# A graph network kernel whose third pass reads its target one-hots back from DRAM, where the second pass has stored them

## The chip, the cores and the metric

The kernel runs on one core of a Trainium2 chip. The metric is the device time of one execution in microseconds (us), smaller is better. The core has five engines that run side by side and wait for each other by semaphores only: TensorE (PE in the profile, its weight loads PEld), VectorE (DVE), ScalarE (ACT), GpSimd (POOL) and SyncE (SP), which here only issues DMAs. Transfers between SBUF and DRAM run on 16 DMA engines that all queues share.

## What is computed

Four layers of a graph network follow each other on 12500 nodes of 32 features and 212500 edges, sorted by target. Each layer normalises the node rows, and sums rows of the edges' sources, weighed, at the edges' targets:

```python
h = relu(layernorm(x))
# layer 0
msg = (h @ W_rel)[src, edge_type_16] * edge_weight1
x = x + segment_sum(msg, dst)
# layer 1: two propagations with the same edge weights
prop(v) = segment_sum((-dinv[dst] * edge_weight * dinv[src])[:, None] * v[src], dst)
Tx1 = prop(h);  Tx2 = 2 * prop(Tx1) - h
x = x + relu(h @ W[0] + Tx1 @ W[1] + Tx2 @ W[2] + b)
# layer 2: attention over edges, with a matrix for each of 86 edge types
x = x + relu(segment_sum(a[:, None] * msg, dst) + self_loop)
# layer 3: mean over the neighbours
x = x + segment_sum(h[src], dst) / max(deg, 1)
```

A row of features is 32 numbers. The two `prop` calls of layer 1 have the same sources, targets and weights; only the rows that they pick differ.

## The kernel before

There are five passes over the edges, `s` = 0 to 4 in the code: the first (layer 0), the second and third (the two propagations of layer 1), the attention pass (`s` = 3) and the last (`s` = 4, layer 3). An edge group has 1024 edges, and there are 208 groups. In the second, third and last pass a part of the groups is not gathered but handled as sorted blocks; the others are gathered row by row.

**Sorted blocks.** The first pass sorts 4 groups (4096 edges) at a time by source into 49 buckets of 256 nodes with room for 128 edges ("slots") each. The second and third pass have 26 such blocks, the last has 39. A block is worked off in 8 batches, one of 7 buckets and seven of 6. I call the work on one batch a step: 26 x 8 = 208 steps in the second pass and 208 in the third. In a step `q`

- SP spreads the slots' source numbers over 128 partitions (`lows`, 224 or 192 KB, a ring of 4);
- DVE compares them with the partition's number (`compare_sources`, two instructions), which gives a one-hot for each source;
- PE multiplies that one-hot with the node rows (`pick`), each row kept as three bf16 parts; it runs some steps ahead;
- DVE weighs the picked rows by the edges' weights, and DVE and ACT split the result again into three bf16 parts (high part on ACT, remainder on DVE, middle part on ACT, last part on DVE, in a chain over three steps);
- DVE compares each bucket's targets with 0 to 255 (`compare_targets`, one instruction of 128x256 bf16 for each bucket, 6 or 7 in a step). This gives `to_oh`, a one-hot of the target inside the block's window of 256 nodes, in a ring of 2;
- PE multiplies the split rows with `to_oh` (`send`), and sums over the block in PSUM. After the block's 8 batches DVE adds the 96x256 sums to `big` in SBUF (`add_block`).

**Gathered groups.** For the other 104 groups of the second and third pass GpSimd issues indirect DMAs, 8 for each group of 1024 edges, so 832 in a pass, into 4 slots. Four groups belong to each block; batches 0, 2, 4 and 6 name them:

```python
HIDDEN = {s: {0: 0, 2: 1, 4: 2, 6: 3} for s in (1, 2)}
```

DVE weighs a gathered group and compares its targets (`weigh_group`), PE multiplies (`multiply_group`), DVE adds the window's 80 columns to `big` and frees the slot (`add_group`, whose wait is for PE's last multiplication of that group). ACT lays out the next row numbers as soon as a group has landed.

**Order around the change.** The order of each engine's instructions is written out by hand. In the DVE's step `q` of `pick_weighed` (line 1847 on) it was: sources of batch `q+1`, [third pass, `q` = 2: `add_block`], weigh batch `q`, targets of batch `q-1`, remainder of `q-1`, last part of `q-2`, then

```python
if q - 1 in HIDDEN[s]:
    weigh_group(s, i, HIDDEN[s][q - 1], f=f)
if q - 2 in HIDDEN[s]:
    add_group(s, i, HIDDEN[s][q - 2], f)
```

PE's order in the step that belongs to it is: a piece of the table for the attention pass (third pass only), `pick` of a later batch, `multiply_group`, `send`. So the group that DVE adds at the end of a step is multiplied on PE behind a `pick` that waits for `compare_sources` at the start of the same DVE step.

The third pass also builds that table: as soon as nodes are complete, DVE normalises a pair of node tiles (lines 1982 to 2012), PE makes the products, ACT copies them out and stores 544 or 495 KB a piece (two for each step) from its own queue. SP's queue has only the spread source numbers during a pass. The last pass is like the second with another splitting (no weights), three blocks for a turn, and its own `pick_turn`.

## Time and profile before

| | |
|---|---|
| median of 3 runs | 7773.39 us (7771.03 to 7800.02) |
| the profiled execution | 7774.41 us, of it 7772.6 us span |
| busy: POOL / DVE / PE / ACT | 5242.6 / 4897.8 / 4872.0 / 2357.4 us |
| second pass (DVE's first to last step) | 2331 to 3404 us |
| third pass | 3466 to 4793 us, then the last table pieces to 4873 us |
| attention pass | 4873 us to about 6960 us |
| last pass | 7025 to 7728 us |

How to read the profile: busy time is the time in which an engine executes; idle time before an instruction is put down to what released it. "issue" is time in which the engine waited for nothing that the profile shows, such as its own register and branch instructions. DVEq is DVE's instruction queue: "DVEq L1574" is the semaphore that `add_group` raises when a slot is free. PEclk is the clock that TensorE was granted as a share of 2.4 GHz. Lines are those of the kernel before: L1806 `compare_sources`, L1813 `compare_targets`, L1823 and L1827 `add_block`, L1554 and L2016 `weigh_group`, L1580 `add_group`, L1223 and L1226 `pick`, L1112 `multiply_group`, L1239 `send`, L712 the gathers, L1042 the table stores, L486 the extra semaphore instruction of a double wait.

### The profile page before, as it was taken

The numbers are of one execution on the slowest core, as the hardware profiler recorded it, in microseconds if no ns is written. First come the engines' busy times: TensorE is split into PE (matmuls) and PEld (weight loads), VectorE is DVE, ScalarE is ACT, GpSimd is POOL, SyncE is SP. The second block draws the span as 40 slices with busy tenths as digits, with TensorE's granted clock in tenths as the row PEclk, the third lists the DMA queues.
The fourth block names the chain that finished last, engine by engine and source line by source line (L and its number), as shares of the span: only waits on it lengthen the run. The fifth ranks groups of instructions, "written<-read, shape, count | busy, mean of one in ns | idle before, by whom it ended". The sixth has DMA issues, their size and how long they took to land.

```text
span 7772.6 us, 149728 instructions
## 1 busy us (share of the span) xinstructions
PE 4872.0 (63%) x41375; PEld 4126.7 (53%) x41376; DVE 4897.8 (63%) x16081; ACT 2357.4 (30%) x7420; POOL 5242.6 (67%) x5417
## 2 busy tenths in 40 slices
PE   5333333333337667677777776777777777786777
PEld 2222222222225555566666665677777776775666
DVE  5555555567778888866666665444444444449997
ACT  4444444430012222223544445211121212123322
POOL 2777777777747777757665662677777777756663
PEclk6555555555556776767776776555555555558998
DMA  7111111110012222224656666222222222214443
GB/s 171 14 14 14 14 14 14 14 14 13 13 22 53 52 52 52 52 44 143 213 190 203 201 198 205 59 41 41 41 41 41 41 41 41 41 34 94 100 100 79
DMA packets 464811, 547.95 MB, mean 70 GB/s; under 512 B 217753, under 2 KB 373945, under 8 KB 464629
## 3 DMA queue, kind: packets, MB, share of 16 engines
q0 software_dynamic: 173168, 146.14, 12.7%
q1 hardware_dynamic: 235013, 186.26, 9.4%
q10 hardware_dynamic: 56448, 213.62, 7.0%
q8 instruction: 53, 0.87, 0.0%
q14 instruction: 129, 1.06, 0.0%
HBM read 298.88 MB, written 246.72 MB: 70 GB/s over the span
## 4 chain that ended last, share of the span: by engine, by line
POOL 33%; DVE 21%; issue 18%; PE 17%; DVEq 8%; DMA 2%; ACT 1%; POOLq 0%; ACTq 0%; SPq 0%
POOL arena L712 33%; DVE tbuf L1813 6%; PE ps_agg L1112 6%; DVE tbuf L1806 3%; PE ps_agg L1239 2%; DVEq L1858 2%; DVEq L1561 2%; PE ps_wide L1223 1%; DVE msg L1857 1%; DVE H L1813 1%; DVE msg L1860 1%; PE ps_wide L1342 1%; PE ps_wide L1226 1%; DMA arena<-table,ibuf 1%; DVEq L1863 1%
## 5 line engine op out<-in xcount | busy, mean ns | idle before, releaser
L712 POOL DMA_INDIRECT arena<-table,ibuf x3328 | 3151.3, 947 | 1242.4 <-issue 1129.9
L712 POOL DMA_INDIRECT arena<-nodes,ibuf x2080 | 2088.6, 1004 | 1142.9 <-issue 616.2
L1112 PE MATMUL ps_agg<-mem_b,arena 128*32 128x80 f32 (+1 forms) x3744 | 457.6, 301 | 504.0 <-DVEq L1561 497.7
L1112 PE MATMUL ps_agg<-mem_a,arena 128*32 128x80 f32 (+1 forms) x3744 | 433.0, 291 | 533.0 <-DVEq L1561 511.0
L1112 PEld LDWEIGHTS ps_agg<-mem_b,arena 128*32 128x32 f32 (+1 forms) x3744 | 400.1, 152 | 554.1 <-DVEq L1561 520.9
L1112 PEld LDWEIGHTS ps_agg<-mem_a,arena 128*32 128x32 f32 (+1 forms) x3744 | 378.9, 146 | 592.6 <-DVEq L1561 528.9
L1813 DVE TENSOR_SCALAR tbuf<-iota,at_f 128x256 bf16<-128x256 bf16 x3185 | 680.9, 297 | 0.3 <-PE ps_t L1239 0.3
L1377 PE MATMUL ps_agg<-tbuf,msg 128*64 128x80 f32 x2496 | 373.6, 344 | 337.9 <-DVE msg L2039 337.9
L983 ACT ACTIVATE att<-score 128x8 f32<-128x8 f32 x208 | 43.3, 208 | 1649.1 <-DVE score L2030 1649.1
L1377 PEld LDWEIGHTS ps_agg<-tbuf,msg 128*64 128x64 f32 x2496 | 336.0, 227 | 359.0 <-DVE msg L2039 359.0
L835 ACT ACTIVATE tbuf<-O,tbuf 128x49 bf16<-128x49 bf16 x1664 | 448.5, 363 | 78.3 <-DVE H L1728 78.3
L1580 DVE TENSOR_TENSOR big<-big,ps_agg 32x80 f32 (+1 forms) x468 | 108.2, 231 | 570.5 <-PE ps_agg L1112 555.9
L1806 DVE TENSOR_SCALAR tbuf<-idx_a,pcol 128x768 bf16<-128x768 bf16 (+1 forms) x1040 | 398.9, 425 | 61.1 <-issue 43.2
L2022 DVE TENSOR_TENSOR msg<-arena,ps_z 128x256 f32<-128x256 f32 x208 | 87.6, 421 | 548.6 <-DMA arena<-table,ibuf 548.6
L1239 PE MATMUL ps_t<-tbuf,mem_b 128*96 128x256 bf16 x1560 | 275.4, 325 | 227.5 <-DVE mem_b L1874 176.8
L1239 PE MATMUL ps_t<-tbuf,mem_a 128*96 128x256 bf16 x1625 | 263.2, 307 | 203.9 <-DVE big L1827 108.8
L1372 PE MATMUL ps_wide<-yw,mem_b 80*128 80x33 f32 x1680 | 380.6, 403 | 1.2 <-ACT yw L965 1.2
L1372 PE MATMUL ps_h<-yw,mem_b 80*128 80x33 f32 x1664 | 377.0, 403 | 0.0
L1372 PEld LDWEIGHTS ps_wide<-yw,mem_b 80*128 80x128 f32 x1680 | 366.4, 330 | 19.1 <-issue 17.8
L1372 PEld LDWEIGHTS ps_h<-yw,mem_b 80*128 80x128 f32 x1664 | 362.9, 330 | 17.7 <-issue 17.7
L1554 DVE TENSOR_TENSOR arena<-arena,ew_s 128x256 f32<-128x256 f32 x416 | 176.5, 424 | 308.6 <-DMA arena<-table,ibuf 295.4
L1239 PEld LDWEIGHTS ps_t<-tbuf,mem_b 128*96 128x96 bf16 x1560 | 192.5, 144 | 260.1 <-DVE mem_b L1874 190.4
(388 smaller groups left out, 11745.8 us busy)
## 6 DMA issues: line engine op xcount, KB each, us to landing
table<-tbuf ACTq DMA_DIRECT2D x294, 544.5 KB
idx_a<-lows_d SPq DMA_DIRECT2D x637, 192.0 KB
arena<-table,ibuf POOLq DMA_INDIRECT x3328, 2.4
table<-tbuf ACTq DMA_DIRECT2D x98, 495.0 KB
arena<-nodes,ibuf POOLq DMA_INDIRECT x2080
table<-tbuf SPq DMA_DIRECT2D x25, 1024.0 KB, 4.3
idx_a<-lows_d SPq DMA_DIRECT2D x91, 224.0 KB
nodes<-O SPq DMA_DIRECT2D x7, 224.0 KB, 3.0
```

Source lines behind the costliest of these rows:

```text
L712: nc.gpsimd.indirect_dma_start(out=INTO[s][:, k, c, 0:WIDTH[s]], out_offset=None, in_=TABLE[s], in_offset=bass.IndirectOffsetOnAxis(ap=ibu ...
L835: op = nc.scalar.mul(moved[:, j, 2 + part, :], by_bucket[:, j, :], of)
L1112: last = nc.tensor.matmul(ps_agg[ROW0[s]:ROW0[s] + CHN[s], 0:WIN], narrow[:, k, c, 0:CHN[s]], onehots[b][:, c, :], start=(c == 0), stop=(c ...
L1239: last = nc.tensor.matmul(block_sums[s][0:SPLIT, 0:W2], slot_rows[q % 2][:, k, :], to_oh[s][q % 2][:, k, :], start=(b0 + k == 0), stop=(b0 ...
L1372: last = nc.tensor.matmul(y_own[b][:, c, :], onehot_t[:, c, :], yw[:, :], start=True, stop=True)
L1377: last = nc.tensor.matmul(ps_agg[0:2 * D, 0:WIN], msg[:, c, :], onehots3[k][:, c, :], start=(c == 0), stop=(c == CH - 1))
L1554: V.tensor_tensor(rows, rows, by[:, of].unsqueeze(2).to_broadcast([P, CH, D]), ALU.mult)
L1561: dve.drain()
L1580: V.tensor_tensor(into, into, ps_agg[r0:r1, 0:WIN], ALU.add)
L1806: op = V.tensor_scalar(from_oh[s][q % 2][:, a, 0:n * CAP], lows[q % RING][:, 0:n * CAP], pcol2[:, a:a + 1], None, ALU.is_equal)
L1813: op = V.tensor_scalar(to_oh[s][q % 2][:, k, :], iota2[:, :], at_f[:, e % UNIT[s], b0 + k:b0 + k + 1], None, ALU.is_equal)
L1858: dve.drain()
```

## The change

1. **Second pass: the one-hots are kept.** SP stores every batch of target one-hots to DRAM (`targets_d`), 448 or 384 KB each, 83.5 MB in all, behind the spread of the source numbers 6 batches later (`keep_targets`). DVE waits, before it overwrites one of the two buffers, until the store from it has landed.
2. **Third pass: they come back.** DVE's `compare_targets` and the loading of target numbers (`start_block`) are gone there. SP loads the batch from DRAM into one of the two buffers when PE has sent the batch two before (`return_targets`), and `send` waits for the load (`s_there`).
3. **Second and third pass: order on DVE.** `add_group` moves from step `q-2` to step `q-3`, and ahead of `weigh_group` in that step; `add_block` of the third pass moves from the start of step 2 to behind the remainders (in the second pass it moves ahead of `weigh_group` only). Where no group is weighed, a `drain` stands.
4. **Last pass.** Nothing is read back (`RETURNED` is empty). The one-hots have a ring of 4 in another tile, and the three blocks of a turn are 13 apart instead of neighbours. The order on the engines stays.

The core of the diff:

```diff
+KEPT = BLOCKS[1]
+TO_RING = {1: 2, 2: 2, 4: 4}
+RETURNED = ()
...
+    targets_d = scratch("targets_d", (KEPT * P, NBK * W2), BF16)
...
-        to_oh = {s: [onehot_piece(s, 2 + j).rearrange("p (k w) -> p k w", w=W2) for j in range(2)] for s in BLOCKS}
+        to_oh = {s: [onehot_piece(s, 2 + j).rearrange("p (k w) -> p k w", w=W2) for j in range(2)] for s in (1, 2)}
+        to_oh[4] = [O[:, at:at + n].bitcast(BF16).rearrange("p (k w) -> p k w", w=W2)
+                    for at, n in ((0, 896), (896, 768), (1664, 768), (2432, 768))]
...
+        def block_of(s, n):
+            turn, e = divmod(n, UNIT[s])
+            return e * TURNS[s] + turn
...
-            def spread_lows(h):
-
-                with sp.Fori(0, BLOCKS[(1, 2, 4)[h]]) as i:
-                    for q, (b0, n) in enumerate(BATCHES):
-                        sp.wait_ge(s_from, (BEFORE[h] * NBATCH + q + 1) + i * NBATCH)
-                        sp.dma_start(lows[q % RING][:, 0:n * CAP],
-                                     lows_d[bass.ds(i * (NBK * CAP) + b0 * CAP, n * CAP)].partition_broadcast(P)).then_inc(s_bc[q % RING], 16)
+            def spread_low(h, i, e, q):
...
+            def keep_targets(i, f, q):
+
+                sp.wait_ge(s_made, (f * NBATCH + q + 1) + i * NBATCH)
+                sp.dma_start(kept_rows(i, f, q), to_oh[1][q % 2][:, 0:BATCHES[q][1], :].rearrange("p k w -> p (k w)")).then_inc(s_kept[q % 2], 16)
+
+            def return_targets(h, i, e, q):
+
+                s = (1, 2, 4)[h]
+                sp.wait_ge(s_sent, ((BEFORE[h] + e) * NBATCH + q + 3 - TO_RING[s]) + i * (UNIT[s] * NBATCH))
+                sp.dma_start(to_oh[s][q % TO_RING[s]][:, 0:BATCHES[q][1], :].rearrange("p k w -> p (k w)"),
+                             kept_rows(i, block_of(s, e), q)).then_inc(s_there[q % TO_RING[s]], 16)
+
+            def spread_and_keep():
+
+                late = 6
+
+                def block(i, f, first=False):
+                    for q in range(NBATCH):
+                        spread_low(0, i, f, q)
+                        if q >= late:
+                            keep_targets(i, f, q - late)
+                        elif not first:
+                            keep_targets(i, f - 1, q - late + NBATCH)
...
+            def spread_and_return(h, ahead, soon, returned):
...
+                def turn(i, f, last):
+                    for m in range(n):
+                        if m + ahead < n or not last:
+                            spread(i, f, m + ahead)
+                        if m + soon < n or not last:
+                            give_back(i, f, m + soon)
...
-            spread_lows(0)
+            spread_and_keep()
             store_nodes(1, 1, lambda i: ubuf[1][i])
-            spread_lows(1)
+            for j in range(2):
+                sp.wait_ge(s_kept[j], 16 * (KEPT * NBATCH // 2))
+            spread_and_return(1, 5, 0, (0,))
...
-            spread_lows(2)
+            spread_and_return(2, 4, 2, RETURNED)
...
                     if q == 0:
                         pe.wait_ge(s_sbadd, (BEFORE[h] + e + 1) + i * UNIT[s])
                         carry_wait(pe)
+                    if s == 2:
+                        pe.wait_ge(s_there[q % 2], 16 * (e * (NBATCH // 2) + q // 2 + 1) + i * (16 * NBATCH // 2))
+                        carry_wait(pe)
...
                 def compare_targets(i, e, q):
                     b0, n = BATCHES[q % NBATCH]
-                    dve.wait_ge(s_sent, count(i, e, q, 1))
+                    dve.wait_ge(s_sent, count(i, e, q, 3 - TO_RING[s]))
+                    if s == 1 and (e > 0 or q > 1):
+                        dve.wait_ge(s_kept[q % 2], 16 * ((e * NBATCH + q) // 2) + i * (16 * NBATCH // 2))
+                        carry_wait(dve)
                     for k in range(n):
...
-                        if s == 2 and q % NBATCH == 2 and (q >= NBATCH or not first):
-                            add_block(i, f + q // NBATCH - 1)
                         if q < NBATCH:
                             dve.wait_ge(s_got, count(i, f, q, 3))
...
-                        if goes(q - 1):
+                        if s == 1 and goes(q - 1):
                             compare_targets(i, f, q - 1)
                         dve.drain()
...
+                        if q % NBATCH == 2 and (q >= NBATCH or not first):
+                            add_block(i, f + q // NBATCH - 1)
+                        if q - 3 in HIDDEN[s]:
+                            add_group(s, i, HIDDEN[s][q - 3], f)
+                        if q == 1 and not first:
+                            add_group(s, i, SLOTS - 1, f - 1)
                         if q - 1 in HIDDEN[s]:
                             weigh_group(s, i, HIDDEN[s][q - 1], f=f)
-                        if q - 2 in HIDDEN[s]:
-                            add_group(s, i, HIDDEN[s][q - 2], f)
-                        if q == 0 and not first:
-                            add_group(s, i, SLOTS - 1, f - 1)
-                        if s == 1 and q % NBATCH == 2 and (q >= NBATCH or not first):
-                            add_block(i, f + q // NBATCH - 1)
+                        else:
+                            dve.drain()
...
+                    for j in range(2):
+                        dve.wait_ge(s_kept[j], 16 * (KEPT * NBATCH // 2))
                     dve.wait_ge(s_own, 1)
```

**The order on DVE in the third pass.** First the steps 2 and 3 of a block in the loop of the third pass, on DVE, before: from the weighing of batch 2 (L1860) to the group's window (L1580).

```order
L1860 ISA
L1860 TENSOR_TENSOR msg<-ps_wide,slot_ew 128x192
L1813 TENSOR_SCALAR H<-iota,at_f 128x256 x6
L1869 TENSOR_TENSOR msg<-msg,mem_b 128x192
L1874 TENSOR_TENSOR mem_a<-msg,mem_a 128x7x32
L486 ISA
L486 TENSOR_LOAD meta
L1563 REGISTER_ALU
L1580 REGISTER_ALU
L1580 ISA
L1580 TENSOR_TENSOR big<-big,ps_agg 32x80
```

The same step on DVE in the changed kernel, whose line numbers are others (L1944 weighs, L1953 and L1958 are the remainder and the last part, L1908 adds the block):

```order
L1944 ISA
L1944 TENSOR_TENSOR msg<-ps_wide,slot_ew 128x192
L1953 TENSOR_TENSOR msg<-msg,mem_b 128x192
L1958 TENSOR_TENSOR mem_a<-msg,mem_a 128x7x32
L1902 REGISTER_ALU
L1902 TENSOR_LOAD block_i
L1908 ISA
L1908 TENSOR_TENSOR big<-big,ps_agg 32x256 x3
```

The six target comparisons are gone, the block's sums stand behind the last part instead of at the start of the step, and the group's window is no longer here. It stands a step later, ahead of the next group's weighing; step 3 on DVE in the changed kernel:

```order
L1944 TENSOR_TENSOR msg<-ps_wide,slot_ew 128x192
L1953 TENSOR_TENSOR msg<-msg,mem_a 128x192
L1958 TENSOR_TENSOR mem_b<-msg,mem_b 128x6x32
L495 ISA
L495 TENSOR_LOAD meta
L1652 REGISTER_ALU
L1662 REGISTER_ALU
L1662 ISA
L1662 TENSOR_TENSOR big<-big,ps_agg 32x80
```

**The order on SP in the third pass.** Two steps of the loop before, on SP: one spread of source numbers for each step.

```order
L675 ISA
L675 DMA idx_a<-lows_d 128x896
L674 REGISTER_ALU
L675 ISA
L675 DMA idx_a<-lows_d 128x768
```

The first two steps of the loop now, on SP (L688 is the spread, L706 the load of one-hots into H):

```order
L688 ISA
L688 DMA idx_a<-lows_d 128x768
L705 REGISTER_ALU
L706 ISA
L706 DMA H<-targets_d 128x1792
L687 REGISTER_ALU
L688 ISA
L688 DMA idx_a<-lows_d 128x768
L705 REGISTER_ALU
L706 ISA
L706 DMA H<-targets_d 128x1536
```

Each step now has a second DMA with a wait of its own on SP; the source numbers run 5 batches ahead of the load that stands behind them.

## Rows read from the trace of the kernel before

**Rows 1.** The page's chain of waits over the whole span, shares by engine.

```profile
POOL 33%; DVE 21%; issue 18%; PE 17%; DVEq 8%; DMA 2%; ACT 1%; POOLq 0%; ACTq 0%; SPq 0%
```

**Rows 2.** Busy time by stretch; columns as in the first line. Rows in order of time.

```profile
core 0: us, PE busy (x) PEld busy (x) DVE busy (x) ACT busy (x) POOL busy (x), PEclk, DMA share, GB/s
2331.00:3404.00 1073.00, 754.44 (x5988) 613.45 (x5985) 914.57 (x2881) 241.18 (x1044) 810.51 (x826) 0.71 0.25 51
3466.00:4793.00 1327.00, 976.20 (x13903) 826.07 (x13907) 901.35 (x3280) 607.44 (x1837) 803.55 (x820) 0.73 0.60 190
4793.00:4873.00 80.00, 34.42 (x263) 28.22 (x255) 24.04 (x45) 39.38 (x109) 0.00 (x0) 0.50 0.55 219
4900.00:6900.00 2000.00, 1578.34 (x8224) 1414.84 (x8223) 881.05 (x3005) 392.91 (x1050) 1511.77 (x1603) 0.50 0.22 41
7025.00:7728.00 703.00, 509.12 (x6574) 439.64 (x6575) 667.70 (x2726) 207.58 (x364) 447.44 (x409) 0.98 0.44 98
```

**Rows 3.** Who waited for whom in the third pass; us in total, times, longest.

```profile
POOL arena L712 <- DVEq L1574: 244.5, 84, 4.9
POOL arena L712 <- issue: 236.2, 736, 1.9
...
PE ps_wide L1223 <- DVE H L1806: 183.1, 68, 7.4
DVE big L1580 <- PE ps_agg L1112: 159.1, 79, 2.9
...
PE ps_agg L1239 <- DVE mem_b L1874: 66.5, 58, 4.2
...
PE ps_h L1337 <- ACT ht L1018: 50.3, 46, 2.1
...
DVE big L1823 <- PE ps_agg L1239: 24.7, 10, 4.0
...
PE ps_agg L1239 <- DVE mem_a L1874: 20.1, 25, 1.4
```

**Rows 4.** The chain of waits in the third pass, shares by engine and line.

```profile
by line: issue 12.6%; PE ps_agg L1112 11.7%; PE ps_agg L1239 11.1%; PE ps_wide L1223 8.6%; DVE H L1813 7.3%; PE ps_wide L1342 5.1%; DVE H L1806 3.9%; DVEq L491 2.7%; DVE msg L1860 2.6%; PE ps_wide L1346 2.5%; PE ps_t L1342 2.3%; DVEq L1561 
```

**Rows 5.** Groups of instructions in the third pass, the target comparisons.

```profile
L1813 DVE TENSOR_SCALAR H<-iota,at_f 128x256 bf16<-128x256 bf16 x1274 | 271.3, 298 | 0.0
```

**Rows 6.** Waits in the second pass, POOL's and DVE's.

```profile
POOL arena L712 <- issue: 250.8, 823, 0.3
...
DVE tbuf L1806 <- issue: 35.1, 103, 0.7
...
DVE big L1827 <- issue: 19.6, 25, 0.8
DVE big L1580 <- PE ps_agg L1112: 19.1, 42, 1.1
```

**Rows 7.** Timeline at the end of the second pass: last gather, last weighing.

```profile
3391.96 1.01 POOL L712 DMA_INDIRECT arena<-nodes,ibuf  x1 [0.30 <-issue]
...
3397.30 0.42 DVE L1554 TENSOR_TENSOR arena<-arena,ew_s 128x256 f32<-128x256 f32 x1
```

**Rows 8.** DMA queues in the third pass (q10 ACT, q1 SP, q0 POOL): packets, MB, share.

```profile
q10 hardware_dynamic: 51840, 196.19, 37.7%
q1 hardware_dynamic: 55888, 41.79, 13.3%
q0 software_dynamic: 26272, 13.50, 8.8%
```

**Rows 9.** The page's DMA issues: KB each, median us from issue to landing.

```profile
table<-tbuf SPq DMA_DIRECT2D x25, 1024.0 KB, 4.3
...
nodes<-O SPq DMA_DIRECT2D x7, 224.0 KB, 3.0
```

**Rows 10.** Timeline of the third pass: one send of six buckets on PE.

```profile
4011.57 1.49 PE L1239 MATMUL ps_agg<-H,mem_b 128*96 128x256 bf16 x6
```

**Rows 11.** The gathers from issue to landing, over the whole run.

```profile
DMA to landing us min/median/max: 2.2/2.4/6.2
```

61 lines of the change are left out of this document (47 added, 14 removed).

## The prediction, made before the changed kernel ran

> **What bounds the kernel now.** I began with the page's chain of waits [rows 1]: POOL has a third of it, so the gathers set much of the span. But this is a mean over passes. The busy time by stretch [rows 2] separates them: in the attention pass nothing of the change is present, and I leave it; the second, third and last pass are the ones it touches.
>
> In the third pass (3466 to 4793, 1327 us for 208 steps, 6.38 us a step) no engine is full: PE 976, DVE 901, POOL 804, ACT 607 us busy, the DMA engines 0.60 [rows 2]. The waits [rows 3] show a loop between PE and DVE. DVE waits 159.1 us for PE's group multiplication before it can add the window (L1580), and 24.7 us for the last send before it adds the block (L1823). PE in turn waits 183.1 us for `compare_sources` (L1806), which DVE reaches only after that addition, and 66.5 + 20.1 us for the split rows. POOL waits 244.5 us for DVE to free a slot. The chain of this stretch [rows 4] agrees: PE lines, DVE's L1813 with 7.3%, and no POOL line among the shares printed.
>
> In the second pass (1073 us) POOL is the one that never stops: 823 of its pauses are "issue" of 0.3 us, 250.8 us in total [rows 6], and no wait for a slot stands against them. A gather takes 810.51 / 826 = 0.981 us [rows 2] and the pause 250.8 / 823 = 0.305, so 832 gathers need 1069 us of 1073. DVE is nearly full too: 915 us busy, and short gaps of its own. At the end of the pass [rows 7] the last gather is issued by 3392.97; with a landing of 2.4 us [rows 11] its rows are there at 3395.4, and DVE weighs them at 3397.3. DVE is 1.9 us behind POOL after a whole pass, so neither has anything to give.
>
> In the last pass DVE is busy 667.7 of 703 us [rows 2], and is the bound.
>
> **The third pass, part by part.** Removed on DVE: 1274 comparisons, 271.3 us [rows 5], 1.3 us a step. Moved: `add_group` a step later. Its wait was for a multiplication that stood on PE behind the `pick` of the same step; a step later PE is past it, so most of the 159.1 us goes. `add_block` behind the remainders has more time for PE's last send, and most of the 24.7 us goes; the first send of the next block waits for it, but in the step in which DVE did it before, too, only a few instructions later. Taken singly this is the chain's 7.3% of 1327, 97 us, and 184 us of waits: 281 us. That is more than can be had, since other engines become late next. What each needs for the pass:
>
> - POOL: 832 gathers. At the third pass's 803.55 / 820 = 0.980 us [rows 2] and 0.305 between, 1069 us. In the attention pass, which has no bf16 comparisons on DVE, a gather takes 1511.77 / 1603 = 0.943 us, in the last pass, which is dense with them, 447.44 / 409 = 1.094 [rows 2]. With half the comparisons gone the need is therefore between 832 x 1.248 = 1038 and 1069. I take 1069.
> - PE: 1327 less the waits for DVE (183.1 + 66.5 + 20.1), 1057 us, at the granted clock of 0.73 [rows 2]; the 50.3 us for ACT [rows 3] stay in it. The new wait on `s_there` adds a semaphore instruction to each send, counted below.
> - DVE: 1327 - 159.1 - 24.7 - 271.3 = 872 us. It is no longer near.
> - DMA: 0.598 x 1327 = 794 us of all 16 engines now [rows 8]. ACT's queue moves 196.19 MB in 37.7% of 1327, 500 us, 392 MB a ms; SP's 41.79 MB in 13.3%, 176 us, 237 MB a ms, in smaller packets. The 83.5 MB that come back cost 213 us at the first rate and 352 at the second: 1007 to 1146 us. The returned rows are 3 and 3.5 KB, like the table's 3.8 KB (196.19 MB in 51840 packets), so I take 1007.
>
> The slot that is freed a step later (5 us) does not stop POOL: it comes back to a slot after three other groups, 3 x 8 x 1.285 = 31 us after it filled it, and the slot is busy for landing (2.4), the wait for its turn, and two steps more, some 20 us.
>
> So the pass can't be shorter than 1069 us, 258 less than now. It won't be exactly that: PE and POOL are then equally full, with DVE's uneven steps between them (the pair of tiles is normalised in two steps of four). The two passes with one full engine show what lies between the need and the time: 1073 / 1069, 0.4%, in the second, and 703 / 667.7, 5%, in the last. With two full engines and busy DMAs I take 6%: 1133 us, **194 us less** (5.45 us a step). The bounds are 258 less, and, if only the comparison leaves the chain, 97 less.
>
> The load itself is hidden in this: it is issued when PE has sent batch m-2 and wanted at send m. From the page, 224 KB land in 3.0 us and 1024 KB in 4.3 [rows 9], so 384 or 448 KB in 3.3. If two table stores of 544 KB are in flight, 1.1 MB at 392 MB a ms is 2.8 us before it; with the source numbers (0.8 us at their rate) it lands in about 7 us. Two steps of 5.45 less a send of 1.5 [rows 10] leave 9.4.
>
> **The second pass.** Added on DVE: in 206 of 208 steps a second wait and a semaphore instruction, and a drain in the steps without a group, four more a block, 104 in all. The trace has no row for one alone. The pause before L1806, where a double wait, a semaphore and a drain meet, is 35.1 / 103 = 0.34 us [rows 6]; so one costs between 0 and 0.34, 0 to 70 us. I take 0.1 for a wait (21 us) and 0.05 for a drain (5 us); both are nearer to the lower end, since 206 waits at 0.34 would be 70 us of pause, twice the whole of that row. Removed: the 19.1 us in which DVE waited for the group's product [rows 6]. The sum is **7 us more**; at best POOL allows 2 us less, at worst, with the full 0.34, it is 70 - 19 + 5 = 56 more. The stores take 213 us of DMA beside a share of 0.25 x 1073 = 268: not near full. One is issued when its comparison is done and has to land two steps later, 10.3 us less 1.3 for the comparison between; 3.3 us is what it needs. DVE's last wait for the stores, and SP's before the third pass, cost about 1 us: SP stores the node rows before it waits.
>
> **The last pass.** The waits are for other semaphores with the same partners, and the ring of 4 lets DVE compare before a send whose end it doesn't have to wait for: 0 us, since DVE's own work is the bound and none of it is removed. 35 us of slack (703 - 667.7) is all that could be found there, and the same for a loss.
>
> **The sum**, against the profiled execution's own 7774.4 us (its span and 1.8 around it; the median of the runs is 7773.4, 1 us below): 7774.4 - 194 + 7 + 1 = **7588 us**.
>
> **Rivals.**
>
> 1. *Gathers alone pace the third pass.* For it: POOL sits in 244.5 us of waits that all end in DVE. Then 1069 us, 258 less: 7524. Against: PE's 1057 leave it nothing. If PE's clock rises from 0.73 because its pauses shorten, as in the last pass (0.98), this is what comes.
> 2. *The DMA engines fill up.* At SP's rate the need is 1146 us, and with 5% between need and time 1203: 124 less, 7658. For it: 0.60 now with peaks above; against: the long rows.
> 3. *The comparison was cover, and only its own share of the chain goes*, because DVE then waits for PE elsewhere (for the high part, or at `pick`): 97 less, 7685.
> 4. *The returned one-hots come late, and the kernel is slower.* The place is the wait before `send`. Two steps can't be shorter than a landing and a send, L + 1.5. Today two steps are 12.76, so the third pass loses from L = 11.3 us on; each further us costs 104. At L = 12.5 a step is 7.0 us, the pass 1456, 129 more, and the kernel 7774.4 + 129 + 8 = 7911. For it: gathers landed in up to 6.2 us at worst where the median is 2.4 [rows 11], so landings can stretch 2.6-fold, and 3.3 would be 8.6. Against: 8.6 is still below 11.3.
>
> The Trainium skill speaks for rival 4 ("DMA: Bandwidth & Descriptors", Queues, rings and completion order): a DMA's completion is written only after every earlier write of the same DMA engine, those of other queues included. By that rule a load counts as landed only when the table stores before it are written, and a second pair of stores in flight would add another 2.8 us to the 7. No row of the kernel before shows a large load beside large stores, and this by itself would not reach 11.3.
>
> **Chances.** The forecast 0.45, rival 1 0.15, rival 2 0.18, rival 3 0.12, rival 4 0.07; 0.03 for a third pass as now and the second pass's cost on top. A difference below 0.5% (39 us) can't be told from none here. Faster by more: 0.88, from the first four less a little where the costs of the second pass meet rival 3; within: 0.04; slower: 0.08. The range reaches to the times of rivals 1 and 3 and leaves out rival 4: 7520 to 7695.
>
> **What would show it.** In the changed profile: the third pass from 1327 to about 1133 us, with DVE near 640 us busy, no L1813 in it, and the wait of `add_group` for PE below 30 us. POOL's wait for slots falls from 244.5 to some 50. The second pass stays at 1073 to 1085, with POOL still never waiting. DMA share in the third pass near 0.9, in the second near 0.45. If PE's wait before `send` is put down to a DMA for more than 50 us, rival 2 or 4 has it; if DVE's waits for PE come back at another line, rival 3. The sum is wrong in its second term if DVE's gaps in the second pass grow by more than 30 us, and in its first if POOL waits for slots as before.

## The result, and the profile after

The changed kernel takes **7706.9 us** (median of 4 executions, 7705.3 to 7711.0), the kernel before 7784.7 (4 executions, 7771.0 to 7800.0): ratio 0.9905, 95% interval [0.9891, 0.9919]. The two profiled executions (7774.4 and 7708.5) are 66 us apart, where 186 were forecast, and the time lies above the range. The direction was right, the size was not.

Where the 66 us are. A pass is measured from the start of its first comparison to the end of its last block sum, in us. Each length here and below comes from one profiled execution of its kernel, and whole executions of one kernel differ by more than 20 us (the kernel before: 7771.0 to 7800.0), so a difference of about 10 us in one pass is weak evidence by itself.

| | before | after | change | forecast |
|---|---|---|---|---|
| second pass | 1075.6 | 1088.4 | +13 | +7 |
| third pass | 1327.4 | 1219.7 | **-108** | -194 |
| last pass | 695.7 | 720.8 | **+25** | 0 |
| all between them | | | +4 | +1 |

The busy time of the same stretches after, with the columns of [rows 2] (window, PE, PEld, DVE, ACT, POOL, PEclk, DMA share, GB/s); second, third and last pass:

```profile
2331.00:3419.00 1088.00, 775.72 (x6002) 639.00 (x6001) 925.82 (x2882) 240.98 (x1044) 825.55 (x827) 0.66 0.45 127
3481.00:4701.00 1220.00, 919.26 (x13912) 784.45 (x13912) 655.64 (x1983) 600.83 (x1839) 796.22 (x821) 0.81 0.85 275
...
6933.00:7662.00 729.00, 525.20 (x6576) 454.10 (x6576) 667.55 (x2726) 207.28 (x364) 448.99 (x409) 0.95 0.41 95
```

In the third pass DVE is busy 246 us less, as it should be; the pass is only 108 shorter. The waits of the third pass say what came in place ([rows 3] are those of before; L1888 is the old L1806, L1953 the remainder's subtraction, old L1869, L969 the high part on ACT, old L891, L1321 the send, L1190 the group):

```profile
ACT mem_a L969 <- PE ps_agg L1321: 307.4, 96, 7.8
POOL arena L790 <- issue: 247.1, 768, 1.9
...
PE ps_wide L1301 <- DVE H L1888: 161.8, 89, 7.1
DVE msg L1953 <- ACT mem_a L969: 157.5, 59, 3.8
...
POOL arena L790 <- DVEq L1656: 137.1, 53, 5.1
...
PE ps_agg L1190 <- issue: 62.2, 73, 1.5
...
DVE msg L1953 <- ACT mem_b L969: 56.4, 55, 2.0
...
PE ps_agg L1321 <- DVE big L1908: 10.4, 13, 1.4
...
PE ps_agg L1321 <- DVE mem_b L1958: 3.1, 7, 1.1
```

DVE's 159.1 us for the group's product are gone from the list, and 157.5 + 56.4 = 213.9 us for ACT's high part stand there instead. Before, the largest such row was this one:

```profile
DVE msg L1869 <- ACT mem_b L891: 3.9, 6, 0.8
```

PE waits for the comparison of the sources as before (161.8 against 183.1). The chain of waits of the third pass (compare [rows 4]) has lost DVE's L1813 and gained ACT's copies and stores of the table pieces (L1115, L1120, L1111) and more "issue" (18.7% against 12.6):

```profile
by line: issue 18.7%; PE ps_agg L1190 10.4%; ACT tbuf L1115 7.2%; PE ps_agg L1321 6.4%; PE ps_wide L1301 5.9%; ACTq L1120 3.6%; POOL arena L790 3.5%; DVEq L1947 3.3%; DVE big L1908 2.4%; DVEq L1902 2.3%; ACT tbuf L1111 2.2%; DVEq L500 2.0%;
```

DMA queues of the third pass, for [rows 8]: SP's queue now moves 125 MB, and 34.3% of 1220 us is 418 us, 242 more than before.

```profile
q10 hardware_dynamic: 51849, 196.22, 41.7%
q1 hardware_dynamic: 79506, 125.09, 34.3%
q0 software_dynamic: 26280, 13.50, 8.5%
```

The last packet of a returned batch always ended before the send that needs it. From SP's issue to the end of the last of a batch's 128 packets it is 4.4 us (median of 208; 99% within 6.3), and from there to the send 6.2 us; the shortest margin is 1.7. None of PE's waits in the third pass is put down to a DMA before a send.

**The last pass** does the same work (DVE 667.7 before, 667.55 after), but pauses more. DVE's waits of the stretch, before and then after:

```profile
DVE tbuf L1806 <- PE ps_wide L1226: 17.8, 51, 0.7
DVE tbuf L1806 <- issue: 7.9, 27, 0.3
...
DVE big L1580 <- PE ps_agg L1112: 1.0, 2, 0.8
```

```profile
DVE tbuf L1888 <- PE ps_wide L1304: 22.5, 52, 0.8
DVE tbuf L1888 <- issue: 20.9, 36, 1.6
DVE big L1662 <- PE ps_agg L1190: 8.5, 9, 1.5
```

These rows add up to the 25 us: 13.0 more of "issue", 7.5 more for the group's product (L1580, now L1662) and 4.7 more for `pick` (L1226, now L1304). The new "issue" pauses come once in 56 us, at the first instruction of a turn of the loop; a turn is three blocks, and there are 11. Two from the timeline after:

```profile
7049.02 0.77 DVE L1888 TENSOR_SCALAR tbuf<-idx_a,pcol 128x768 bf16<-128x768 bf16 x2 [1.61 <-issue]
...
7105.01 0.75 DVE L1888 TENSOR_SCALAR tbuf<-idx_a,pcol 128x768 bf16<-128x768 bf16 x2 [1.25 <-issue]
```

The queue that brings instructions carried 51 packets of 8192 bytes more in this pass, nearly five for each of the 11 turns. Its row in the last pass, before and after:

```profile
q14 instruction: 11, 0.09, 0.0%
```

```profile
q14 instruction: 62, 0.51, 0.2%
```

### The profile page after: what moved, and what is told of

Same layout as the page of the kernel before. It is cut to its first block, busy times and chain, and to the rows that moved or that the text cites. A ratio compares the mean times of both kernels' runs of the same rounds, so it can differ in the third digit from the quotient of the medians.

```text
span 7706.6 us, 150447 instructions
## 1 busy us (share of the span) xinstructions
PE 4857.4 (63%) x41375; PEld 4129.9 (54%) x41376; DVE 4655.3 (60%) x14781; ACT 2348.9 (30%) x7420; POOL 5252.2 (68%) x5417
## 4 chain that ended last, share of the span: by engine, by line
POOL 35%; issue 20%; DVE 19%; PE 12%; DVEq 8%; ACT 3%; DMA 2%; ACTq 1%; POOLq 0%; SPq 0%
POOL arena L790 35%; PE ps_agg L1190 4%; DVE O L1898 3%; DVE tbuf L1898 3%; DVE tbuf L1888 3%; DVEq L1942 2%; DVE msg L1941 2%; ACT tbuf L1115 1%; DVEq L1947 1%; PE ps_agg L1321 1%; PE ps_wide L1301 1%; DMA arena<-table,ibuf 1%; DVE arena L1636 1%; DVE msg L1953 1%; DVEq L1643 1%
## 5 line engine op out<-in xcount | busy, mean ns | idle before, releaser
L790 POOL DMA_INDIRECT arena<-nodes,ibuf x2080 | 2097.0, 1008 | 1069.3 <-issue 615.9
L1190 PE MATMUL ps_agg<-mem_a,arena 128*32 128x80 f32 (+1 forms) x3744 | 471.3, 307 | 560.6 <-DVEq L1643 510.7
L1190 PE MATMUL ps_agg<-mem_b,arena 128*32 128x80 f32 (+1 forms) x3744 | 471.7, 308 | 509.7 <-DVEq L1643 495.1
L1190 PEld LDWEIGHTS ps_agg<-mem_a,arena 128*32 128x32 f32 (+1 forms) x3744 | 412.1, 156 | 620.4 <-DVEq L1643 528.7
L1190 PEld LDWEIGHTS ps_agg<-mem_b,arena 128*32 128x32 f32 (+1 forms) x3744 | 412.2, 155 | 559.2 <-DVEq L1643 519.0
L1888 DVE TENSOR_SCALAR tbuf<-idx_a,pcol 128x768 bf16<-128x768 bf16 (+1 forms) x1040 | 397.7, 424 | 72.6 <-issue 50.1
L1898 DVE TENSOR_SCALAR O<-iota,at_f 128x256 bf16<-128x256 bf16 x1911 | 406.5, 293 | 0.0
L1662 DVE TENSOR_TENSOR big<-big,ps_agg 32x80 f32 (+1 forms) x468 | 108.1, 231 | 454.8 <-PE ps_agg L1190 391.1
L969 ACT CAST mem_a<-msg 128x224 bf16<-128x224 f32 x208 | 74.4, 358 | 878.8 <-PE ps_t L1321 520.6
L904 ACT COPY ibuf<-idx_a 128x8 int32 x208 | 39.7, 196 | 931.2 <-DMA arena<-table,ibuf 929.0
L1212 PE MATMUL ps_wide<-O,not_before 128*128 128x392 bf16 x156 | 82.3, 528 | 358.6 <-DVE H L1810 358.6
```

What stands on the lines that cost most here:

```text
L790: nc.gpsimd.indirect_dma_start(out=INTO[s][:, k, c, 0:WIDTH[s]], out_offset=None, in_=TABLE[s], in_offset=bass.IndirectOffsetOnAxis(ap=ibu ...
L1190: last = nc.tensor.matmul(ps_agg[ROW0[s]:ROW0[s] + CHN[s], 0:WIN], narrow[:, k, c, 0:CHN[s]], onehots[b][:, c, :], start=(c == 0), stop=(c ...
L1662: V.tensor_tensor(into, into, ps_agg[r0:r1, 0:WIN], ALU.add)
L1888: op = V.tensor_scalar(from_oh[s][q % 2][:, a, 0:n * CAP], lows[q % RING][:, 0:n * CAP], pcol2[:, a:a + 1], None, ALU.is_equal)
L1898: op = V.tensor_scalar(to_oh[s][q % TO_RING[s]][:, k, :], iota2[:, :], at_f[:, e % UNIT[s], b0 + k:b0 + k + 1], None, ALU.is_equal)
```

## The experiments

Line numbers of an experiment can differ by a few from those of after. "Placed" is explained at f1. Ten of the 18 experiments met a disturbed chip, on which the kernel before itself takes 10375 to 10520 us. Their ratios compare with the kernel before on the same chip, and their pass lengths hold only beside each other. Five of these kernels were run again on undisturbed chips (f2 as r1, f3 as g1, f4 as h1, h3 as n1, m2 as n2); f1, the changed kernel with nothing but its loop placed, was not. Pass lengths are in us, second / third / last.

| kernel | time | ratio to before | passes |
|---|---|---|---|
| before | 7774.4 profiled | | 1075.6 / 1327.4 / 695.7 |
| after | 7706.9 | 0.9905 [0.9891, 0.9919] | 1088.4 / 1219.7 / 720.8 |
| r1 order alone, placed | 7787.8 | 1.0001 [0.9989, 1.0013] | 1086.8 / 1327.8 / 705.7 |
| g1 return alone, placed | 7700.4 | 0.9901 [0.9882, 0.9920] | 1099.3 / 1219.4 / 698.2 |
| h1 send first, placed | 7683.9 | 0.9872 [0.9856, 0.9889] | 1090.4 / 1215.1 / 696.3 |
| h2 h1, bounds early | 7683.5 | 0.9869 [0.9853, 0.9886] | 1091.4 / 1217.6 / 697.2 |
| n1 16 columns, placed | 7657.2 | 0.9829 [0.9807, 0.9851] | 1088.5 / 1189.5 / 698.9 |
| n2 h1, fewer copies | 7664.9 | 0.9839 [0.9818, 0.9861] | 1088.3 / 1201.6 / 699.2 |
| p2 early comparison, placed | 7669.1 | 0.9843 [0.9827, 0.9860] | 1087.7 / 1192.6 / 699.4 |
| p1 n2 and p2 | 7683.7 | 0.9858 [0.9841, 0.9874] | 1089.9 / 1208.7 / 700.6 |

On disturbed chips:

| kernel | time | ratio to before | passes |
|---|---|---|---|
| e1 order alone | 10680.6 | 1.0284 [1.0267, 1.0301] | 1567 / 2073 / 1009 |
| e2 return alone | 10407.4 | 1.0027 [1.0008, 1.0046] | 1424 / 1940 / 980 |
| e3 16 columns loaded | 10516.4 | 1.0122 [1.0103, 1.0141] | 1590 / 1913 / 965 |
| e4 16 columns stored | 10493.0 | 1.0103 [1.0067, 1.0139] | 1590 / 1914 / 965 |
| f1 after, placed | 10664.2 | 1.0130 [1.0095, 1.0164] | 1604 / 1921 / 1023 |
| f2 order alone, placed | 10776.8 | 1.0242 [1.0207, 1.0277] | 1577 / 2066 / 1024 |
| f3 return alone, placed | 10517.2 | 0.9996 [0.9982, 1.0010] | 1472 / 1917 / 1008 |
| f4 send first, placed | 10638.0 | 1.0107 [1.0073, 1.0142] | 1601 / 1904 / 1009 |
| h3 as n1 | 10509.9 | 1.0101 [1.0077, 1.0125] | 1591 / 1906 / 1000 |
| m2 as n2 | 10490.1 | 1.0094 [1.0072, 1.0116] | 1586 / 1882 / 970 |

### Which edit gives the gain: e1, e2, f2, f3, g1, r1

The order alone, on the kernel before:

```diff
-                        if s == 2 and q % NBATCH == 2 and (q >= NBATCH or not first):
-                            add_block(i, f + q // NBATCH - 1)
 ...
+                        if q % NBATCH == 2 and (q >= NBATCH or not first):
+                            add_block(i, f + q // NBATCH - 1)
+                        if q - 3 in HIDDEN[s]:
+                            add_group(s, i, HIDDEN[s][q - 3], f)
+                        if q == 1 and not first:
+                            add_group(s, i, SLOTS - 1, f - 1)
                         if q - 1 in HIDDEN[s]:
                             weigh_group(s, i, HIDDEN[s][q - 1], f=f)
-                        if q - 2 in HIDDEN[s]:
-                            add_group(s, i, HIDDEN[s][q - 2], f)
```

Return alone is the same edit the other way, on the changed kernel. f2 and r1 have 92 drains for the placing, f3 and g1 have 14 and 110.

> The kernel before with nothing but the new order on DVE in the second and third pass (group sums a step later, block sum behind the remainders, the drains that go with it); target one-hots are compared in all three passes as before. Theory A, the loop through all engines sets the third pass (send on PE, high part on ACT, remainders on DVE, the next comparison, the next pick): the order takes out DVE's wait for the group's product (159.1 us), but that time reappears partly as a wait for the high part, so the pass goes from 1327 to about 1270 us, the kernel to about 7715. Theory B, DVE's wait was not on that loop and only moves: the pass stays within 15 us of 1327 and DVE waits at the remainder line for ACT by over 120 us. In both the second pass stays at 1074 to 1078 and the last pass at 703.

> The changed kernel with DVE's old order in the second and third pass; the one-hots are kept and returned as in the change. Theory A: 1.3 us of DVE a step are gone, but the wait for the group's product is back; third pass about 1275 us, second pass 1088, last pass 729, kernel about 7765. Theory B, the comparison is the whole gain: third pass within 15 us of the changed kernel's 1219, kernel about 7705. Theory C, neither edit gives anything without the other: 1310 or more, kernel about 7800.

> The kernel before with DVE's new order alone, and 92 drains in the branch not taken so that the last loop lies within three stretches. On a chip like that of the first profiles: theory A (the loop through all engines sets the third pass) 1327 to about 1270 us, kernel about 7715; theory B (the wait only moves) within 15 us of 1327. On a chip whose gathers land late, as in the first four experiments (DVE waits of 10 to 15 us for rows, kernel before 10375 us): the order costs time, since every slot is freed a step later; the kernel is about 2.5% slower than before, nearly all of it in the second and third pass.

> The changed kernel with DVE's old order, and 14 and 110 drains in branches not taken, so that the loops of the third and the last pass lie within three stretches (without them the third pass showed 126 instruction packets on q14). On a chip like that of the first profiles: theory A 1275 us for the third pass, kernel about 7735; theory B, the comparison is the whole gain, 1220 and 7680. On a chip whose gathers land late: faster than before by 1 to 2%.

> The kernel of f3 once more (one-hots returned, DVE's old order, loops placed), to see the chip state of the first profiles, in which the kernel before takes 7773 us and PE has no pauses of 2 us between single multiplications. There, theory A: third pass 1275 us, kernel about 7735; theory B (the removed comparison is the whole gain): third pass 1220 us, kernel about 7680. In the other state: within 0.5% of the kernel before, as f3.

> The kernel before with DVE's new order alone and its last loop placed (the kernel of f2), for the chip state of the first profiles. Theory X, the two edits take away the same time, so that either would do: the third pass is about 1240 us, the kernel about 7690. Theory Y, only the removed comparison shortens DVE's part of the loop and the order gives nothing by itself: within 15 us of 1327, the kernel within 0.3% of the kernel before. In both the second pass is 1070 to 1078 us and the last 698.

Measured: the third pass is 1327.4 (before), **1327.8 (order alone), 1219.4 (return alone)** and 1219.7 (both). The order gives nothing there, with or without the returned one-hots; the comparison is the whole gain. Theory Y holds, and B of f3 and g1. Theory A was wrong in both. How the wait moves is seen in r1's rows of the third pass:

```profile
ACT mem_a L891 <- PE ps_agg L1239: 387.7, 101, 7.4
...
POOL arena L712 <- DVEq L1574: 234.7, 73, 7.6
...
PE ps_wide L1223 <- DVE H L1806: 168.8, 107, 7.4
DVE H L1813 <- PE ps_agg L1239: 90.2, 52, 2.8
```

DVE no longer waits 159.1 us for the group's product, but 90.2 for the send at the next comparison of targets (not at the remainder, where theory B of e1 had looked for it), and PE and POOL wait nearly as long as before (183.1, 244.5). g1, which has the returned one-hots and the old order, shows the other side:

```profile
DVE big L1662 <- PE ps_agg L1190: 248.3, 100, 4.4
```

With the comparison gone DVE waits 248.3 us for the group's product. The new order takes that row away, 213.9 us for ACT's high part come in its place, and the pass is 1219 us either way.

In the second pass r1 is 11 us longer than before (1086.8), though none was expected: a gather takes 825.3 / 828 = 0.997 us in r1, 0.982 before. In the whole kernel it does not show: over ten executions r1 takes as long as the kernel before (1.0001 [0.9989, 1.0013], about 10 us to either side). The returned one-hots' stores and waits cost 24 us with the old order (1099.3, a gather 0.979), and both together 13. In g1 the gathers are done at 3399.5 us, and DVE needs until 3428.6: there DVE sets the pass, and the new order hides DVE's waits at the price of slower gathers. Rows of the gathers in the second pass, before, r1, g1 and after:

```profile
L712 POOL DMA_INDIRECT arena<-nodes,ibuf x826 | 810.9, 982 | 251.8 <-issue 250.8 <-ACT ibuf L826 0.9
```

```profile
L712 POOL DMA_INDIRECT arena<-nodes,ibuf x828 | 825.3, 997 | 252.5 <-issue 252.5
```

```profile
L790 POOL DMA_INDIRECT arena<-nodes,ibuf x828 | 811.0, 979 | 259.9 <-issue 254.2 <-DVEq L1656 5.4 <-ACT ibuf L904 0.3
```

```profile
L790 POOL DMA_INDIRECT arena<-nodes,ibuf x827 | 826.5, 999 | 252.1 <-issue 242.6 <-DVEq L1656 8.2 <-ACT ibuf L904 1.2
```

Why a gather takes 15 ns more beside the new order was not tried. On disturbed chips the new order costs time: e1 and f2 are 2.8 and 2.4% slower than before. f3 was expected 1 to 2% faster there and is level (0.9996). The expectations of f2 and f3 call this the late landing of gathers. The traces do not bear that out: in e1's trace DVE waits for no gathered row in the second and third pass, and its long waits (up to 19.0 us) are for the picked rows, with no releaser in the profile.

### Stores and loads of 16 columns: e3, e4, h3, n1

e3, h3 and n1 load 16 columns of a batch (the edit shown); e4 stores 16 columns and loads the first block's one-hots at full size each time. All four leave out part of the one-hots, so their sums are wrong and they serve for times only.

```diff
-                sp.dma_start(to_oh[s][q % TO_RING[s]][:, 0:BATCHES[q][1], :].rearrange("p k w -> p (k w)"),
-                             kept_rows(i, block_of(s, e), q)).then_inc(s_there[q % TO_RING[s]], 16)
+                columns = slice(0, BATCHES[q][1] * W2 if whole else 16)
+                sp.dma_start(to_oh[s][q % TO_RING[s]][:, 0:BATCHES[q][1], :].rearrange("p k w -> p (k w)")[:, columns],
+                             kept_rows(i, block_of(s, e), q)[:, columns]).then_inc(s_there[q % TO_RING[s]], 16)
```

> The changed kernel, whose loads in the third pass bring only 16 of the 1536 or 1792 columns of a batch of one-hots, except in the first block; the block sums are then made with stale one-hots. The waits and the number of loads stay. Theory A, the loop through the engines sets the pass: it stays within 15 us of 1219 although q1 moves some 80 MB less. Theory D, full DMA engines or late landings set it: the pass falls by over 40 us, towards the 1133 that was forecast.

> The changed kernel, whose stores in the second pass keep only 16 columns of a batch, except in the first block; the third pass loads the first block's one-hots every time, at full size. Theory S, the stores slow the gathers: a gather goes back from 0.998 to about 0.981 us and the second pass from 1088 to about 1075. Theory W, the added waits and drains on DVE cost it: gather and pass stay at 0.998 and 1088. The third and last pass stay as in the changed kernel, 1219 and 729.

> The changed kernel with its last loop placed, whose loads in the third pass bring only 16 of the 1536 or 1792 columns of a batch, except in the first block (block sums with stale one-hots; the number of loads and all waits stay): the experiment e3 for the chip state of the first profiles. Theory D, the DMA engines at 0.85 set the third pass: it falls by over 40 us from 1219, towards 1133. Theory T, ACT's work on the table pieces sets it: within 15 us of 1219. In the changed kernel the last packet of a returned batch ends 4.4 us after its issue and 6.2 us before the send (medians of 208), which speaks for T.

> The kernel of h3 once more, for the chip state of the first profiles: only 16 of the 1536 or 1792 columns of a batch are loaded in the third pass, so block sums use stale one-hots. Theory D (DMA): the third pass falls by over 40 us from 1219. Theory T (ACT's piece work): within 15 us of 1219.

Measured in n1: the third pass is 1189.5 us, 30 less than 1219.7. The row of that stretch:

```profile
3483.00:4673.00 1190.00, 901.27 (x13912) 772.46 (x13912) 655.60 (x1984) 600.51 (x1839) 794.66 (x821) 0.82 0.70 215
```

That is between the two theories. With the DMA engines down at 0.70 the pass still needs 1190 us, so the traffic is not the whole of what holds it, but it costs 30 us. The pause before the group on PE (L1190 <- issue) falls from 62.2 to 36.7 us and POOL's wait for slots from 137.1 to 108.8. On the disturbed chips e3 and e4, which share a chip, have the same third pass (1913.2 and 1913.5) with small and with full loads, and the same second pass (1590.4, 1590.2) with full and with small stores. That speaks for theory W as to the size of the stores. But the gathers there (0.970 us) were not as in the undisturbed second pass, so e4 doesn't settle it.

### Where DVE's loops lie: f1, and all placed kernels

```diff
                         dve.sem_inc(s_gfree, 1)
+                    for _ in range({1: 0, 2: 88, 4: 0}[s]):
+                        dve.drain()
                 dve.drain()
```

> The changed kernel with 88 drains more in DVE's program, in a branch that is not taken, between the third pass and the attention: nothing that runs is changed, only where DVE's loops lie. Counted in the compiled program, the last pass's loop has 380 instructions of 64 bytes and lies across four stretches of 8192 bytes in the changed kernel (51 instruction packets more than before on q14, and a pause of 1.3 us on DVE at each new turn of the loop), and within three here. Theory F, DVE fetches its loop anew at every turn because it does not fit where it lies: q14 goes from 61 packets back to about 10 in the last pass, the pauses at the start of a turn go, and the pass is about 25 us shorter than without the move (704 against 729 on a chip like that of the first profiles). Theory G, the ring of four or the order of the blocks costs it: nothing changes.

Measured: f1 shows 11 packets on q14 in the last pass, against 60 to 62 in e1, e2, e3, e4 and after. The chip was disturbed, and there the time does not show it: the last pass has 1022.8 us in f1 and 964.6 to 1009.0 in the four unplaced kernels, on another chip. So the time comes from kernels on undisturbed chips that are placed and have the changed kernel's last pass: 696.3 (h1), 697.2, 698.2, 698.9, 699.2, 699.4 and 700.6 us against 720.8 after and 695.7 before. In h1 DVE's waits are those of before again:

```profile
DVE tbuf L1891 <- PE ps_wide L1304: 17.6, 50, 0.7
DVE tbuf L1891 <- issue: 8.2, 28, 0.3
...
DVE big L1665 <- PE ps_agg L1190: 1.5, 2, 1.3
```

So theory F holds: in h1 neither the ring of four nor the order of the blocks is undone, and packets and pauses are gone. Not all of the 25 us is shown to be its work. r1 is placed too, has the last pass of before and shows 10 packets, but its last pass takes 705.7 us, with this row:

```profile
DVE big L1580 <- PE ps_agg L1112: 8.2, 9, 1.0
```

That is the changed kernel's 8.5 us without any fetching. The pauses themselves are 13 us, and 720.8 lies 15 to 24 us above the placed kernels, r1 included.

A count that fits all cases: number DVE's instructions of 64 bytes in the compiled program, add 64 to the number of the loop's first and last one, and see how many stretches of 128 instructions (8192 bytes) the loop touches. Three: no packets of its own (before's three loops, after's second and third, every placed one; lengths 258 to 380). Four: nearly five packets a turn. These are the last loop of after (3690 to 4069, 51 packets more in 11 turns), those of e1 and e2, and e2's third pass (2236 to 2514, with 126 packets and 24 turns, where f3 with 14 drains more ahead has 10). The 64 was chosen to make these cases agree, and 63 to 65 would do; the trace shows no addresses, so this is a fit and not a measured rule. The order alone shifts the last loop as well: e1's has the 378 instructions of before, only 36 further on.

### What paces the third pass: f4, h1, h2, m2, n2, p1, p2

f4 and h1 (second hunk), h2 (both; `multiply_group` there takes `windows`):

```diff
+                        windows = bounds_of_group(pe, turn_group(s, i, f, HIDDEN[s][q]))[1] if q in HIDDEN[s] else None
                         if q + 3 < NBATCH or not last:
                             pick(i, f, q + 3, sums)
 ...
+                        if s == 2:
+                            send(i, f, q)
                         if q in HIDDEN[s]:
                             multiply_group(s, i, HIDDEN[s][q], f)
-                        send(i, f, q)
+                        if s != 2:
+                            send(i, f, q)
```

> As f1, and in the third pass PE sends a batch before it multiplies the group of that step, not after it. Theory A: send, high part, remainders, next comparison and next pick are one loop, and the group (1.2 us of pause and 1.3 us of multiplication in half of the steps) is taken out of it: DVE's waits for the high part (157.5 + 56.4 us) fall below half and the third pass is 40 to 80 us shorter than 1219. Theory H, PE's total work and clock set it: the pass stays within 15 us.

> The kernel of f4 once more (the whole change, last loop placed, in the third pass PE sends before it multiplies the group), for the chip state of the first profiles. Since g1 gave 1219 us for the third pass with DVE's old order, as the changed kernel did with the new one, the wait only moved from the group's product to the high part; both end when PE has done the group and the send of a step. Theory A: with the send ahead of the group, DVE's waits for the high part (157.5 + 56.4 us) fall below half and the pass is 40 to 80 us shorter than 1219, the kernel about 7625. Theory H, PE's total work and clock set it: within 15 us of 1219, kernel about 7683 (the changed kernel less 23 for the placed loop).

> As h1, and in the second and third pass PE reads the bounds of a group into registers ahead of the pick of that step, where it mostly waits for DVE's comparison anyway, not between pick and group; there the trace shows a pause of 1.2 to 1.3 us with no releaser in 73 cases (62.2 us in the third pass). Theory A: the pause goes from PE's loop and the third pass is 20 to 60 us shorter than in h1. Theory B: the reading takes as long wherever it stands; within 10 us of h1.

Measured: in h1 PE's pause before the group falls from 62.2 to 6.9 us and DVE's waits for the high part from 213.9 to 149.1 (theory A wanted less than half), but the pass is 1215.1, only 5 less. Two rows of h1 show waits that stand in the way of the rest, and its timeline shows the second:

```profile
PE ps_agg L1321 <- DVE big L1911: 72.2, 25, 3.7
ACT mem_a L969 <- issue: 79.5, 53, 4.6
```

```profile
4008.55 0.86 ACTq L1120 DMA_DIRECT2D table<-tbuf  x2
4009.68 0.35 ACT L969 CAST mem_a<-msg 128x192 bf16<-128x192 f32 x1 [1.31 <-issue]
```

PE now waits 72.2 us, once a block, for DVE's block sum, where it waited 10.4: the change had moved that sum behind the remainders, and the send that stands first meets it too early. All kernels with the send ahead have this wait (76.3 in h2, 80.7 in n2, 74.0 in p1). A kernel with the send ahead and the block sum early was not run. And ACT, whose high part could start sooner, is still issuing the two stores of a table piece. h2 is within theory B's 10 us of h1, 1217.6. Theory A failed in both. The time is what H expected, which does not show that H's cause, PE's work and clock, sets the pass.

m2 and n2 leave out ACT's copies of a value that already stands in the staging buffer, and have h1's order:

```diff
-                for a in range(2):
+                for a in range(2) if h < 2 else ():
                     nc.scalar.copy(row_stage[a][h % 2][:, 0:n, PAIR:PAIR + D],
```

> As h1 (send ahead of the group, last loop placed), and ACT copies the own columns into the staged table rows only for the first two of four pieces: the third and fourth are staged in the same two buffers, where the same values still stand. That is 0.87 us less for ACT in every second piece, 78 us of its 606 in the third pass. Theory T, ACT's work on the pieces is the link that holds the high part back: the pass goes from 1215 to 1150 to 1190 us. Theory D, the DMA engines hold it, or theory H, PE at its granted clock: within 10 us of 1215.

> The kernel of m2 once more (send ahead of the group, half of the copies of O into the staged table rows), for the chip state of the first profiles. Theory T: third pass 1150 to 1190 us, kernel 7625 to 7660. Theory D or H: third pass within 10 us of the 1215 of h1, kernel about 7683. On the disturbed chip the same step, f4 to m2, took 22 us off the pass.

Measured in n2: 1201.6, 13 less than h1 for 67 us less of ACT (605 to 538). That lies between T and its rivals. m2 is 22 us shorter than f4 in this pass, on another disturbed chip.

p2 compares the sources of batch q+2 right behind the weighing, ahead of DVE's wait for the high part; p1 has n2's edits too. The core of the edit:

```diff
-                        if goes(q + 1):
+                        if s == 1 and goes(q + 1):
                             compare_sources(i, f, q + 1)
 ...
                             compare_targets(i, f, q - 1)
+                        if s == 2 and goes(q + 2):
+                            compare_sources(i, f, q + 2)
                         dve.drain()
```

> The changed kernel with the last loop placed, the send ahead of the group, half of the O copies, and in the third pass DVE compares the sources of batch q+2 right behind the weighing of batch q, not those of q+1 at the start of the step: so the pick of the next batch no longer waits for the high part. Theory A, the loop send, high part, remainders, comparison, pick is what is left: PE's wait for the comparison (150.2 us in n2) falls below 40 and the third pass goes from 1201 to 1120 to 1160 us, kernel about 7600. Theory P, something else paces it (DMA traffic, the gathers' slots): the wait turns up elsewhere and the pass stays within 15 us of 1201. On a chip on which PE pauses between multiplications: about 1% slower than before, as f4 and m2.

> The changed kernel with the last loop placed and only the earlier comparison of the sources in the third pass (as in p1). Theory A: third pass from 1219 to 1140 to 1180 us, kernel about 7630. Theory P: within 15 us of 1219, kernel about 7683.

Measured: PE's wait for the comparison is gone, 161.8 to 7.3 us, and p2's pass is 1192.6, 27 less. That is short of theory A (1140 to 1180) and past P's 15 us. Waits of p2's third pass:

```profile
ACT mem_a L969 <- PE ps_agg L1321: 231.3, 86, 7.0
POOL arena L790 <- DVEq L1656: 112.1, 56, 5.2
DVE msg L1957 <- ACT mem_a L969: 100.9, 59, 3.0
...
PE ps_h L1419 <- ACT ht L1096: 76.1, 46, 3.4
...
PE ps_agg L1190 <- issue: 70.0, 72, 1.8
...
PE ps_wide L1301 <- DVE H L1888: 7.3, 2, 7.1
```

Of the 155 us, 27 come off the pass. PE gets back 24 in longer multiplications (busy 943 against 919, granted clock 0.77 against 0.81, p2's row below), 29 in its wait for ACT's `ht`, 33 in its wait for the last part of the split rows (35.7 against 3.1), and the rest in smaller ones.

```profile
3487.00:4679.00 1192.00, 943.32 (x13906) 809.59 (x13910) 653.57 (x1983) 602.19 (x1839) 796.77 (x820) 0.77 0.86 281
```

And the edits don't add up: p1, with n2's and p2's, has 1208.7, longer than either, as its theory P had it. The new order, the send ahead, the early bounds, the halved copies and the early comparison each take a wait or work out of the third pass. They gave 0, 5, -2, 13 and 27 us, of which the 5 and the -2 are too small to be told from chance.

The best of the exact kernels are n2 and p2, 7664.9 and 7669.1 us, 0.984 of before. Against the changed kernel n2 has 18 us less in the third pass and 22 in the last, p2 27 and 21; the part in the last pass comes with the placed loop.

## Why the prediction was wrong

**The third pass, -194, was -108.** The step that failed is "the third pass, part by part": that the comparison's 97 us of chain and the 184 us of waits both come off until the fullest engine stops it, 6% above its need. Of the two edits only the comparison paid, 108 us for its 271 us of work; the chain's own 7.3% had said 97. The order's waits, 159.1 and 24.7 us, were counted as 184 us of gain and were worth nothing (r1: 1327.8): DVE, let past the group's product, stood next before the send (90.2 us in r1) or the high part (213.9 us after). This is rival 3, to which I gave 0.12; it asked for 1230 and its sign ("DVE's waits for PE come back at another line") is in the rows: before PE's send, by way of ACT. The busy need, 1069 us for POOL and 1057 for PE, never became the bound: in the changed kernel POOL still waits 137.1 us for slots where 50 were forecast. The 6% was taken from two passes that each have one full engine. In the third pass no engine is full, a batch is handed round between engines that each work in order, and its time is 14% above POOL's need; that this handing round is the reason is my reading, and no run shows it by itself.

**The other terms of the DMA** were near. The returned one-hots cost 242 us of the engines, between the 213 and 352 of the bounds; the share is 0.85 where 0.9 stood. The load is in time: 4.4 us where 7 were estimated, with 6.2 to spare. So rival 4 is out. By the rule of the Trainium skill that the prediction cited ("DMA: Bandwidth & Descriptors", Queues, rings and completion order) landings beside the table stores could have been longer. The packets show 6.3 us at the 99th percentile; when the last of the writes counted as done the trace does not show. Rival 2, full DMA engines, is a part and not the bound: 30 us of the pass go when the loads are cut (n1).

**The second pass, +7, was +13.** The forecast had 26 us for waits and drains on DVE and took off 19 for its wait for the product. The runs split it otherwise: the returned part alone, without drains, costs 24 (g1), and the new order takes 11 of that back. What the forecast left out is the slower gathers beside the new order (0.982 to 0.997 us; r1's pass is 11 us longer). All these are differences of single executions. "POOL never waits" held, but for 8.2 us.

**The last pass, 0, was +25.** The step was "0 us, since DVE's own work is the bound and none of it is removed". The work was indeed the same; what changed is where the loop lies in DVE's program. The pauses that came with it are 13 us of the 25, and the placed kernels lie 15 to 24 us below 720.8. The new ring and the new order of the blocks are in seven placed kernels whose last pass is 696.3 to 700.6 us, so they are not the cause.

**The sum** with what was measured: 7774.4 - 108 + 13 + 25 + 4 = 7708.4, the profiled execution's 7708.5. That only says the parts are complete. With the last loop placed the change would be worth some 80 to 90 us (an estimate: 66 and the 15 to 24 above), near rival 3's 7685. h1, which is that kernel with a new PE order that gave 5 us, has 7683.9.

**What stays open.** The third pass has 1219.7 us where POOL needs 1069. The traffic is worth 30, half of ACT's copies 13, the early comparison 27, and the last two together do not add. What PE's wait for the late block sum costs (72.2 us in h1) was not tried. Which of PE's granted clock, the "issue" time (18.7% of the chain) and the handing round sets the rest is not settled.

## What to carry to other kernels

- The chain's own share of what is removed (here 7.3%, 97 us, for a gain of 108) forecast the gain better than the waits did; this is one case. A wait that stands in a loop through several in-order engines is not a gain to be added: ask what that engine waits for next, and count it only when no other wait ends on the same instruction.
- A reordering that only moves a wait should be tried by itself. Here it gave nothing in the pass it was made for, came with slower gathers in another, and made the kernel 2.4 to 2.8% slower on disturbed chips. There POOL waits longer for slots with the new order (537.3 us in f1's second pass) than with the old (401.3 in f3's).
- After an edit anywhere ahead of a tight loop look at the instruction queue's packets. The loop may now be fetched anew at each turn, and padding in a branch that is not taken can stop that.
- Before one instruction is moved earlier, look for what it will now wait for. The send ahead of the group met a block sum that the same change had made later, and 72.2 us of waiting for it came in.
